# Splitting the last product of a four-tile FFN finish across two units of the TensorE order

## The reference

```python
x = x + _L0_attn_ref(_layernorm(x), w_qkv, w_out)
# _L0_ffn_ref(h = _layernorm(x)), added to x:
base_out   = h @ base_W.T + base_b
shared_out = (h @ shared_A.T) @ shared_B.T
gate       = softmax(h @ router_W.T + router_b)        # top 2 of 6 kept, made to sum to 1
routed_out = sum over experts of gate_e * (h @ A_e.T) @ B_e.T
x = x + base_out + shared_out + routed_out
```

## Time and profile before

| | |
|---|---|
| median of 3 runs | 296.71 us (296.19 to 296.82) |
| the profiled execution | 296.31 us, of which 294.6 us are its span |
| PE busy | 278.1 us, 94% |
| ACT busy | 268.9 us, 91% |
| DVE / POOL busy | 138.6 us, 47% / 65.5 us, 22% |
| granted TensorE clock | 1.0 |

### The profile page before, as it was taken

One profiled execution on the slowest core, in us unless ns is written; L12 is line 12 of the kernel. 1 busy time (PEld: TensorE's weight loads), 2 busy tenths in 40 slices (PEclk: granted clock), 3 DMA queues, 4 the chain that ended last, 5 costly groups with the idle time before them and its releaser, 6 DMA issues.

```text
span 294.6 us, 7507 instructions
## 1 busy us (share of the span) xinstructions
PE 278.1 (94%) x2998; PEld 102.8 (35%) x2998; DVE 138.6 (47%) x419; ACT 268.9 (91%) x306; POOL 65.5 (22%) x139
## 2 busy tenths in 40 slices
PE   7979988999999999999999999999999999999996
PEld 2634332222222222132233134445433435444344
DVE  6875957686051558517171036522113262541055
ACT  8668899899999999999998999999999998999921
POOL 3647465423403021040030121010101010103002
PEclk9999999999999999999999999999999999999999
DMA  6343443004700000000001700001000000000000
GB/s 208 109 119 97 118 127 93 0 3 111 185 28 2 4 0 2 0 0 2 2 0 30 209 17 2 2 2 38 0 3 2 2 3 28 10 2 2 21 0 18
DMA packets 15400, 11.81 MB, mean 40 GB/s; under 512 B 2097, under 2 KB 14370, under 8 KB 15362
## 3 DMA queue, kind: packets, MB, share of 16 engines
q1 hardware_dynamic: 14738, 10.71, 13.1%
q0 software_dynamic: 192, 0.39, 0.5%
q10 hardware_dynamic: 432, 0.20, 0.3%
HBM read 3.95 MB, written 1.05 MB: 17 GB/s over the span
## 4 chain that ended last, share of the span: by engine, by line
PE 49%; ACT 26%; issue 14%; DVE 6%; DMA 2%; SPq 0%; ACTq 0%; DVEq 0%
ACT pbuf L758 26%; PE po L1223 22%; PE ps L1198 14%; PE pm L1239 1%; PE pm L1233 1%; PE pm L1285 1%; PE ps L1239 1%; PE ps L1347 1%; DMA qst<-parts 1%; PE pm L1245 1%; PE pm L1291 1%; PE pm L1299 1%; DMA xs<-x_dram 1%; DVE rest L851 1%; PE pm L1295 1%
## 5 line engine op out<-in xcount | busy, mean ns | idle before, releaser
L758 ACT ACTIVATE pbuf<-ps 128x1024 f32<-128x1024 f32 (+1 forms) x280 | 253.5, 1079 | 7.2 <-PE ps L1198 6.3
L1223 PE MATMUL po<-pbuf,va 128*9 128x256 f32 (+3 forms) x1792 | 143.8, 426 | 1.2 <-DVE oq L831 0.8
L1198 PE MATMUL ps<-qst,kst 64*128 64x256 bf16 (+3 forms) x896 | 97.3, 297 | 8.3 <-ACT pbuf L758 3.9
L685 POOL TENSOR_SCALAR_AFFINE_SELECT pbuf<-pbuf 128x256 f32<-128x256 f32 (+1 forms) x104 | 47.8, 482 | 194.1 <-ACT pbuf L758 193.7
L1198 PEld LDWEIGHTS ps<-qst,kst 64*128 64x128 bf16 x896 | 30.6, 94 | 106.8 <-ACT pbuf L758 80.3
L1223 PEld LDWEIGHTS po<-pbuf,va 128*9 128x9 f32 x1792 | 35.1, 89 | 55.4 <-issue 33.1
L831 DVE STREAM_TRANSPOSE oq<-po 128x256 f32<-128x256 f32 (+1 forms) x24 | 12.9, 539 | 66.4 <-PE po L1223 66.1
L851 DVE TENSOR_TENSOR rest<-pm,sinT 32x512 f32<-32x512 f32 x16 | 11.0, 687 | 0.3
L1347 PE MATMUL ps<-kst 128*128 128x512 bf16 (+1 forms) x38 | 9.8, 391 | 0.0
L798 DVE BATCH_NORM_STATS2 stats<-xs 128x6 f32<-128x128 f32 x32 | 7.1, 281 | 2.5 <-DMA xs<-x_dram 1.4
L1239 PE MATMUL ps<-xnT,wqkv 128*128 128x256 f32 (+1 forms) x24 | 8.0, 462 | 0.0
(11 more groups left out here) (158 smaller groups left out, 189.5 us busy)
## 6 DMA issues: line engine op xcount, KB each, us to landing
qst<-parts SPq DMA_DIRECT2D x18, 128.0 KB, 2.6
kst<-parts SPq DMA_DIRECT2D x18, 128.0 KB, 2.4
xs<-x_dram SPq DMA_DIRECT2D x4, 256.0 KB, 3.2
cosT<-rope_c_dram SPq DMA_DIRECT2D x3, 256.0 KB, 3.8
sinT<-rope_s_dram SPq DMA_DIRECT2D x3, 256.0 KB, 4.1
out_dram<-xs SPq DMA_DIRECT2D x3, 256.0 KB, 2.3
kst<-parts SPq DMA_DIRECT2D x8, 64.0 KB, 2.4
qst<-parts SPq DMA_DIRECT2D x7, 64.0 KB, 2.0
```

Of the source, the lines that this page charges most:

```text
L685: ins = nc.gpsimd.affine_select(out=edge, in_=edge, compare_op=ALU.is_ge, fill=0.0, base=0, pattern=[[0, edge.shape[1]], [1, P]], channel_ ...
L758: nc.scalar.activation(probs[:, :, 0:width], ps[:, SLOT[u], :, 0:width], ACT.Exp, scale=SCALE).then_inc(exp_ready, 1)
L1198: ins = nc.tensor.matmul(ps[:, SLOT[u], e, place:place + n], side(kst, e)[:, g * 2 + pair, key:key + P], side(qst, e)[:, g * 2 + pair, q:q ...
L1223: ins = nc.tensor.matmul(po[32 * j:32 * j + DH + 1, output(i, g, q0, n)], va[:, kt, g * GH + j, :], pbuf[:, u % NPB, at:at + n], start=blk ...
```

## The change

F of finishes 0, 1 and 2 is given to PE in two parts. At the unit of F (148, 193, 243) PE issues `base` alone. The four `wup` matmuls follow behind the scores of the next unit and ahead of the values due there. DVE is told that `pm` is full at the end of the second part. No matmul is added or removed, nothing else moves, and the two-tile finishes keep F whole. The diff also prepares other products for halving; `HALVED` names only F, and only where it is the last product of its unit with four tiles.

```diff
+HALVED = ("F",)
+HALVED_FROM = FIRST_UNIT[2]
+def halved(job, u):
+    name, c = job
+    tiles = FINISHES[c][1] if name in FINISH else TC
+    return name in HALVED and u >= HALVED_FROM and tiles == TC
...
-            def job(name, c):
-
-                if AWAITED[name, c] is not None:
+            def job(name, c, half=None):
+
+                if AWAITED[name, c] is not None and half != 1:
                     pe.wait_ge(job_fed, FED[AWAITED[name, c]])
...
                 elif name == "F":
-                    base(product, nt)
-                    for t in range(nt):
+                    if half != 1:
+                        ins = base(product, nt)
+                    for t in range(nt if half != 0 else 0):
                         ins = nc.tensor.matmul(product[:, tile(t)], lowT[0:RD + 1, t, :], wup[:, :], start=False, stop=True,
                                                skip_group_check=True)
-                ins.then_inc(act_full if (name, c) in READ_BY_ACT else job_full, 1)
+                if half != 0:
+                    ins.then_inc(act_full if (name, c) in READ_BY_ACT else job_full, 1)
...
                 scores(u)
...
+                for name, c in begun:
+                    job(name, c, 1)
+                begun = []
                 for b in due.get(u, ()):
                     values(b)
-                for name, c in PRODUCTS_AT.get(u, ()):
-                    job(name, c)
+                mine = PRODUCTS_AT.get(u, ())
+                for n, (name, c) in enumerate(mine):
+                    if n + 1 == len(mine) and halved((name, c), u):
+                        job(name, c, 0)
+                        begun = [(name, c)]
+                    else:
+                        job(name, c)
```

More of the change, by code:

```diff
@@ L1232, in base, with project, project_v @@
                 for t in range(nt):
-                    nc.tensor.matmul(product[:, t * P:(t + 1) * P], feat[:, t * P:(t + 1) * P], wbase[:, :],
-                                     start=t == 0, stop=False, skip_group_check=True)
-            def project(p, name, product):
+                    ins = nc.tensor.matmul(product[:, t * P:(t + 1) * P], feat[:, t * P:(t + 1) * P], wbase[:, :],
+                                           start=t == 0, stop=False, skip_group_check=True)
+                return ins
+            def project(p, name, product, half=None):
                 which = ("K", "KS", "Q", "QS").index(name)
-                return nc.tensor.matmul(product, wqkv[:, which, :], xnT[:, chunk(p) % 2, local(p)], start=True, stop=True)
-            def project_v(p, product):
+                at, n = local(p).start, PREPS[p][1] * P
+                first, last = (0, n) if half is None else (half * n // 2, (half + 1) * n // 2)
+                return nc.tensor.matmul(product[:, first:last], wqkv[:, which, :],
+                                        xnT[:, chunk(p) % 2, at + first:at + last], start=True, stop=True)
+            def project_v(p, product, tiles=None):
                 at = local(p).start
-                for t in range(PREPS[p][1]):
+                for t in range(PREPS[p][1]) if tiles is None else tiles:
                     ins = nc.tensor.matmul(product[:, t * P:(t + 1) * P], xnT[:, chunk(p) % 2, at + t * P:at + (t + 1) * P],
@@ L1259, in job @@
                 nt = FINISHES[c][1] if name in FINISH else TC
+                tiles = range(nt) if half is None else range(half * nt // 2, (half + 1) * nt // 2)
                 if (name, c) == ("Q", 2):
@@ L1276, in job @@
                 elif name in ("K", "KS", "Q", "QS"):
-                    ins = project(c, name, product)
+                    ins = project(c, name, product, half)
                 elif name == "V":
-                    ins = project_v(c, product)
+                    ins = project_v(c, product, tiles)
                 elif name == "B":
@@ L1283, in job @@
                     pe.wait_ge(ffn_in, 16 * 6)
-                    for t in range(nt):
+                    for t in tiles:
                         ins = nc.tensor.matmul(product[:, tile(t)], feat[:, tile(t)], wout[:, :], start=True, stop=True)
@@ L1412, in _ @@
             pe.wait_ge(zeroed, 1)
-            due = blocks_by_unit()
+            due, begun = blocks_by_unit(), []
             for u in range(len(UNITS)):
```

## The result

The changed kernel took 296.88 us (median of 12 runs, 296.58 to 297.37) against 296.45 us for the kernel before (12 runs, 296.06 to 296.82). The ratio over all runs is 1.0018, 95% interval 1.0010 to 1.0026: +0.53 us (0.30 to 0.77), where the two medians differ by 0.43. It is a small loss, clear of zero, and just under the 0.2% (0.59 us) that the prediction used as its bound. The profiled execution took 296.72 us with a span of 295.0 us.

What follows compares the result with a forecast made beforehand. The prediction took ACT's stream of exps as the bound, with a late PE costing time where it leaves ACT idle. Three cuts by 0.20 us make +0.60, so 296.71 + 0.60 = 297.3 us, range 296.5 to 297.9.

Steps and rivals of the forecast that it cites:

- The place of the bound: At F of finish 0 the chain leaves PE for ACT at unit 150's exp, 161.24 us, not at unit 149's.
- the second exp: ACT's exp of unit 150 at finish 0: forecast to start 0.20 us later, at 161.44 instead of 161.24.
- the first gap: ACT's idle time before unit 149's exp at finish 0, 0.52 us: forecast to close and add to the next gap.
- The scores of unit 149 earlier: On PE, base gives way after 1.09 us; these scores end at 159.01, before ACT is free at 159.42.
- The cost of the cut: On PE from F to unit 150's scores: one more border and product-run head, 3.80 against 3.60, +0.20 us per F.
- The upper bound: At each F, wup to values costs the 0.1 us of other borders, making a cut cost 0.20 us.
- the border wup-values: On PE, wup followed directly by values, seen in no row of before: forecast between 0 and 0.1 us.
- What hangs on the end of F: wup ends 0.52 us later; feat has 1.2 us of cover, the qst DMAs for unit 160 0.9: no cost.
- rival 3: F's late end reaches unit 160's scores or O of finish 3, adding 0.5 us: 297.8 us; chance 0.08.
- The half-price cut: At F the cut costs half or nothing: +0.0 to +0.3 us, 296.7 to 297.0; chance 0.35.
- The kept first gap: At the three F, exp(149) and its counterparts end earlier and that time stays won: 1.92 us, 294.8 us; chance 0.07.
- The time: Whole kernel: median 296.71 us plus 0.60 for three cuts makes 297.3 us, +0.20%.

Runs made afterwards that it cites:

- Experiment 1: Kernel before with F uncut but one unit later (149, 194, 244): ratio 1.0016 against before, 0.5 us slower.
- Experiment 2: Changed kernel with F cut once more, two wup matmuls ahead of the values and two behind: ratio 1.0045 against the kernel before, 1.3 us slower.
- experiment 3: Changed kernel with wup behind the values of the next unit, not ahead of them: ratio 1.0021 against the kernel before.
- Experiment 6: Changed kernel with second parts 7, 7, 5 units later and jobs moved, finish 0's store ahead of the stacking DMAs: 1.0150 against before, 4.4 us slower.
- experiments 4 and 7: Changed kernel, second parts 7, 7, 5 units later, jobs and store moved: 0.9966 against before; only finishes 0, 1 cut (157, 200), O and store moved: 0.9955.

## Why the prediction was right, by its own steps

- **The place of the bound.** Right: the chain still leaves PE for ACT at the second exp, and the first gap was never on it. Experiment 1 closed that gap in another way, and gained nothing either.
- **The scores of unit 149 earlier.** Right. All three first gaps closed; base gave way after 1.09 us.
- **The cost of the cut.** I took 0.20 per F between bounds of 0.10 and 0.20. Measured were 4.23 against 4.03 at finish 0, 4.24 against 4.05 at the two others, 0.58 in all for my 0.60. The upper bound was an argument from likeness, not a row, and it held. Experiment 2 doubled it by another cut (+0.39 at finish 0), experiment 3 left it as it was with wup elsewhere. At the border wup-values the first value pass starts 0.205 us behind the last pass of wup, where passes of one run are 0.112 apart, so the border costs 0.09. The rule on tiling modes in the Trainium skill's "TensorEngine Tiling (Array Packing)", section Key Properties, has a drain there; the trace agrees, and its 0.09 us is a price that the page does not name. The head of the run costs the other 0.10 (0.213 to its second pass). That this is the load of the first weights, which can't hide behind the scores, is argued and not shown; no experiment tells it from another cause.
- **What hangs on the end of F.** Right, so rival 3 fell. The delay was 0.52 us at finish 0 (DVE's addition began 2.93 us behind the scores of unit 148, before 2.41), and it was covered. Experiment 6 shows that the queue that I had named as the next to feel it is real: with the store 5.0 us later than before (165.30 against 160.34), the kernel took 5.4 us more than with the store moved away.
- **The rivals.** The half-price cut (0.35) fell with the chain's 1.09 for wup and with experiment 2. The kept first gap (0.07) fell with experiment 1. Its condition, a PE with slack, is what experiments 4 and 7 made, and there the sign turned.
- **The time.** 297.3 was 296.71 + 0.60. The change measured 0.53 by the ratio and 0.56 in the traces from the first exp to the last values. The median of 296.88 lies 0.43 under my 297.31: 0.26 because the kernel before itself ran at 296.45 over twelve runs, and 0.17 because the medians differ by 0.43 and not by 0.60. That a difference under 0.2% can't be told from none was wrong: with twelve runs each the interval is 0.30 to 0.77 us. Since the forecast sat on that bound, it was luck on which side of it the result fell.

## What to carry to other kernels

Follow the chain to the exact instruction at which the waiting engine is released; if the piece that is moved still stands ahead of it, the gap only changes place. A cut of a long insertion costs its two surcharges of 0.1 us each in any case. It pays only when the engine has time to run ahead between the parts (here nine and seven units, 1.3 us gained with two finishes cut and one product moved), and even then not the whole gap comes back. Before moving an end later, list every queue behind it, and what the freed place is needed for next.

## What the runs showed of the hardware that I had not expected

In experiment 6 PE stood idle for 4.51 us, and its clock fell just after it had begun again. These are a stretch inside the wait, the one behind it, and the next (busy us and instructions of PE, PEld, DVE, ACT, POOL, then the granted clock, DMA share, GB/s):

```profile
168.60:173.00 4.40, 0.00 (x0) 0.00 (x0) 0.00 (x0) 1.06 (x2) 1.46 (x4) 1.00 0.55 148
173.30:176.60 3.30, 3.30 (x24) 0.74 (x18) 0.00 (x0) 2.15 (x3) 0.00 (x0) 0.50 0.64 178
176.70:182.00 5.30, 4.91 (x78) 1.90 (x76) 2.67 (x4) 5.30 (x7) 0.00 (x0) 1.00 0.00 0
```

In the wait the granted clock still reads 1.00. In the middle stretch it is 0.50, the 1.2 GHz level, though PE is busy throughout, and the same eight value passes take 1.90 us and not 1.05. To the start of the scores behind them it is 1.83 us (173.91 to 175.74) and not 0.98. These 0.85 us more are the 0.86 us gap of ACT in that experiment: one wait of 4.5 us cost a second one.
